# Two-layer graph and expert network, one core: filler products on TensorE in the graphs without a shared expert

## The chip, the cores and the metric

The kernel runs on one core of one Trainium2 chip. The metric is the device time of one execution in microseconds. The engines that matter here are TensorE (PE), VectorE (DVE) and ScalarE (ACT); GpSimd (POOL) does normalisation scalars and scatters, SyncE (SP) issues loads. "Granted clock" is the share of TensorE's full clock that the chip let it have in a stretch, as the profiler records it: 1.00 is 2.4 GHz, 0.50 is 1.2 GHz.

## The reference

The whole program is two layers of graph network and expert network over 16 graphs of 512 nodes with 256 features. The change lies in the third of its four parts, the attention over the graph's edges, into which the shared expert of the fourth part has been woven:

```python
def _L1_gnn_ref(X, A, Wp, bp, C):            # 8 heads of 32 features
    Xp = jnp.einsum('bnd,hdk->bhnk', X, Wp) + bp[None, :, None, :]
    Xc = jnp.einsum('bhnk,hjk->bhnj', Xp, C)
    attn = jnp.tanh(A[:, None] * jnp.einsum('bhnj,bhmj->bhnm', Xc, Xp))
    Xh = jnp.einsum('bhnm,bhmk->bhnk', attn, Xp)
    return jax.nn.relu(jnp.moveaxis(Xh, 1, 2).reshape(X.shape[0], X.shape[1], -1))
...
# in _L1_ffn_ref
shared = jax.nn.silu(xf @ sw1) * (xf @ sw3) @ sw2
```

## The kernel before

Four phases follow one another: the first graph network, the first experts, `attention_phase`, and the second experts with the final sums. Only `attention_phase` is touched. It takes the graphs b = 0 to 15 in order, and a graph in eight units u = 0 to 7, each with two halves c = 0 and 1. A unit is one block of 128 tokens for four of the eight heads. The work of a half unit goes round three engines:

- PE computes `scores` (L1408, 32 rows by 512 columns, six products) into half of the four banks `c_p_s`;
- DVE multiplies them with the adjacency in `products` (L1901, into `c_att`, two buffers that alternate by unit);
- ACT takes the tanh in place (L1699);
- PE sums the heads' outputs in `values` (L1421) once per unit, one unit behind.

The order on each engine is written out by hand. On PE a half unit is: wait for the product of DVE, `scores` of the next unit, then in half 0 `side_a(u)` and `values(u-1)`, in half 1 `side_b(u)`. The side functions hold everything else: the next graph's transposes and projections (`turn` L1428, `wide` L1440, `turn_back` L1434, `project_c` L154 to L156), the router of the graph before (`logits` L1452), the count of expert members (`count_before` L937 and L939), and the shared expert: `wide` with `ws1` and `ws3` in units 5, 6 and 7, and `down` (L1459) in units 0 and 1 of the graph after. They use three PSUM banks, `c_p_w[0..2]`; z and w name the two that swap with the graph's parity.

The shared expert is computed here for the first eight graphs alone (`OWN = 8`):

```python
going_up, going_down = post and b - 1 < OWN, late and b - 2 < OWN
```

`post` is true from graph 1 on, `late` from graph 2 on. So graphs 1 to 8 hold the upward products, graphs 2 to 9 the downward ones, and from graph 9 (10 for units 0 and 1) those places are empty. The other graphs' shared expert is computed in a later phase.

DVE's `products(b, h, u, c)` at c = 0 has two waits: `av_done` of two units before, that is until `values` has read the buffer `c_att` that it will overwrite, and `s_done`, its scores. DVE's own side work stands behind the two products of a unit.

Of the kernel before, what the change touches and what calls it, by code (L numbers as in the profile page):

```python
# [42 lines left out]
GRP = 2  # L43
# [1118 lines left out]
def attention_phase(nc, a, m, sb):  # L1162
# [3 lines left out]
    with ExitStack() as ctx:  # L1166
# [233 lines left out]
        def _(pe):  # L1400
# [36 lines left out]
            def wide(w, f, src, bank, done, last_of=False):  # L1437

                for k in range(KD):
                    mm = pe.matmul(p_s[:, bank, :] if last_of else p_w[:, bank, :], w[:, k, f * P:(f + 1) * P], src[:, k, :],  # L1440
                                   start=(k == 0), stop=(k == KD - 1))
                mm.then_inc(done, 1)
# [13 lines left out]
            def down(c, bank):  # L1456
# [3 lines left out]
                                       start=(i == 0), stop=(i == KHS - 1))  # L1460
                mm.then_inc(down_done, 1)

            def project_first():

                pe.wait_ge(xn_ready, 1)
                turn(xn, 0, 1, tr_done)
                turn(xn, 1, 2, tr_done)
                pe.wait_ge(xt_ready, KD)
                pe.wait_ge(s_w, 16 * NL)
                pe.wait_ge(init, 4)  # L1470
                wide(wp, 0, xt, 0, xpt_done)
                wide(wp, 1, xt, 1, xpt_done)
                pe.wait_ge(xpt_ready, 1)
                turn_back(xpf[:, 0], 2, xp_done)
                pe.wait_ge(xp_ready, 1)
                pe.wait_ge(xpt_lo, 1)
                pe.wait_ge(cd_split, 2)
                project_c(0, 0, 2)
                pe.wait_ge(xpt_ready, 2)
                pe.wait_ge(xpt_lo, 2)  # L1480
                project_c(0, 1, 0)
                pe.wait_ge(xct_lo, 1)
                turn_back(xpf[:, 1], 2, xp_done)
                scores(0, 0, 0, 0)
                scores(0, 0, 0, 1)

            def graph(q, h, first, last):
                b = 2 * q + h
                post = not is_at(b, 0)
                late = post and not is_at(b, 1)  # L1490
                going_up, going_down = post and b - 1 < OWN, late and b - 2 < OWN
                z, w = h, 1 - h

                def side_a(u):
                    if u == 0 and late:
                        pe.wait_ge(member_ready, b - 1)
                        if going_down:
                            pe.wait_ge(sh_ready, KHS * (b - 2) + 2)
                        else:
                            pe.wait_ge(xp_ready, GRP * b + 2)  # L1500
                        count_before(pe, m, count, member, count_done)
                    if u == 1 and post:
                        pe.wait_ge(ot_ready, GRP * b)
                        if late:
                            pe.wait_ge(r2_step, R2 * (b - 2) + 2)
                        else:
                            pe.wait_ge(xp_ready, GRP * b + 2)
                        turn_back(ot[:, 1], 2, back_done)
                    if u == 2 and not last:
                        pe.wait_ge(xn_ready, b + 2)  # L1510
                        if going_down:
                            pe.wait_ge(x4_ready, TB * (b - 2) + 1)
                        else:
                            pe.wait_ge(xct_lo, GRP * b + GRP)
                        turn(xn, 0, z, tr_done)
                        if post:
                            pe.wait_ge(x3_ready, GRP * b)
                        else:
                            pe.wait_ge(xp_ready, GRP)
                        turn(xn, 1, 2, tr_done)  # L1520
                    if u == 3 and post:
                        pe.wait_ge(xn3_ready, b)
                        if last:
                            pe.wait_ge(xct_lo, GRP * b + GRP)
                        turn(xn3[:, 1 - h], 0, z, tr3_done)
                        turn(xn3[:, 1 - h], 1, 2, tr3_done)
                    if u == 4 and not last:
                        pe.wait_ge(xpt_ready, GRP * (b + 1) + 1)
                        if post:
                            pe.wait_ge(xt3_ready, KD * b)  # L1530
                        turn_back(xpf[:, 0], 2, xp_done)
                    if u == 5:
                        pe.wait_ge(ot_ready, GRP * b + 1)
                        if not last:
                            pe.wait_ge(xpt_ready, GRP * (b + 1) + 2)
                        turn_back(ot[:, 0], z, back_done)
                    if u == 6 and going_up:
                        pe.wait_ge(x3_ready, GRP * b + 1)
                        wide(ws3, 0, xt3, z, up_done)
                    if u == 7 and going_up:  # L1540
                        pe.wait_ge(xp_ready, GRP * (b + 1) + 2)
                        wide(ws1, 1, xt3, 2, up_done)

                def side_b(u):
                    if u == 0 and going_down:
                        pe.wait_ge(hs_ready, KHS * (b - 1))
                        pe.wait_ge(xct_lo, GRP * b + GRP)
                        down(0, z)
                    if u == 1 and going_down:
                        down(1, w)  # L1550
                    if u == 2 and not last:
                        pe.wait_ge(xt_ready, KD * (b + 2))
                        if going_down:
                            pe.wait_ge(x4_ready, TB * (b - 1))
                        elif post:
                            pe.wait_ge(x3_ready, GRP * (b - 1) + 1)
                        else:
                            pe.wait_ge(xpt_ready, GRP)
                        wide(wp, 0, xt, w, xpt_done)
                    if u == 3 and not last:  # L1560
                        if post:
                            pe.wait_ge(xt3_ready, KD * (b - 1) + 1)
                        wide(wp, 1, xt, z, xpt_done)
                    if u == 4 and post:
                        pe.wait_ge(xt3_ready, KD * b)
                        if last:
                            pe.wait_ge(x3_ready, GRP * (b - 1) + 1)
                        logits(xt3, w)
                    if u == 4 and not last:
                        pe.wait_ge(xp_ready, GRP * (b + 1) + 1)  # L1570
                        pe.wait_ge(xpt_lo, GRP * (b + 1) + 1)
                        project_c(1 - h, 0, 2)
                    if u == 5 and going_up:
                        pe.wait_ge(sg_ready, b)
                        wide(ws1, 0, xt3, w, up_done)
                    if u == 5 and not last:
                        pe.wait_ge(xct_lo, GRP * (b + 1) + 1)
                        turn_back(xpf[:, 1], 2, xp_done)
                    if u == 6 and not last:
                        pe.wait_ge(xpt_lo, GRP * (b + 1) + 2)  # L1580
                        if going_up:
                            pe.wait_ge(sh_ready, KHS * (b - 1) + 1)
                        elif post:
                            pe.wait_ge(sg_ready, b)
                        project_c(1 - h, 1, w)
                    if u == 7 and going_up:
                        pe.wait_ge(hs_ready, KHS * (b - 1) + 1)
                        wide(ws3, 1, xt3, z, up_done)

                for u in range(UNITS):  # L1590
                    for c in range(2):
                        pe.wait_ge(prod_ready, 2 * (UNITS * b + u) + c + 1)
                        if u + 1 < UNITS:
                            if u + 1 == T and c == 0:
                                pe.wait_ge(xct_lo, GRP * b + 2)
                            scores(b, h, u + 1, c)
                        elif not last:
                            scores(b + 1, 1 - h, 0, c)
                        if c == 0:
                            side_a(u)  # L1600
                            if u > 0:
                                values(b, h, u - 1)
                            elif post:
                                values(b - 1, 1 - h, UNITS - 1)
                        else:
                            side_b(u)
# [762 lines left out]
```

## Time and profile before

| | |
|---|---|
| median of 3 runs | 2244.68 us (2244.51 to 2255.48) |
| profiled execution, its own time | 2249.72 us |
| span of its instructions | 2247.9 us |
| mean granted TensorE clock over the span | 0.935 |
| PE, DVE, ACT, POOL busy | 2065.9, 1537.5, 1249.5, 1065.9 us |
| attention phase, first to last product of DVE | 1022.4 to 1755.3 us of the span |

The profiled execution is 5.0 us longer than the median of the timed ones. PE's busy time includes the latency of each product, so 92% busy is not 92% of what PE could do. A unit is measured here from the start of DVE's first product of that unit to the start of the first product of the next unit.

### The profile page before, as it was taken

The page shows a single profiled execution, that of the slowest core. Times are in us where ns is not written, and L with a number is a line of the kernel's source. Part 1 is how long each engine was busy: PE and PEld are TensorE (multiplying, and loading weights), DVE is VectorE, ACT ScalarE, POOL GpSimd, SP SyncE. Part 2 cuts the span into 40 slices and gives each one's busy share as a digit, 9 for nine tenths or more (in the row PEclk, how much of TensorE's full clock was granted, in tenths as well). Part 3 has the DMA queues.
Part 4 walks back from the last instruction along what each step waited for, and adds up shares of the span by engine and source line. Part 5 has one row for each costly group of instructions (what it writes and reads, how often), then busy time and mean ns, then how long its engine had stood idle before and what let it go on. Part 6 is the DMA issues. An engine that isn't in the chain of part 4 may idle for free. (4 is left out here: it accounts for less than half of the span.)

```text
span 2247.9 us, 38345 instructions
## 1 busy us (share of the span) xinstructions
PE 2065.9 (92%) x12128; PEld 1509.9 (67%) x12128; DVE 1537.5 (68%) x3332; ACT 1249.5 (56%) x1870; POOL 1065.9 (47%) x1266
## 2 busy tenths in 40 slices
PE   7999999947999999958999999998999789999986
PEld 6988888846888888843444444444444478878853
DVE  6777777744666666645777778767776557767759
ACT  4444444404666666646676666755655357767630
POOL 3455555541333333326455545556432447777740
PEclk9999999968999999988999999978776899999998
DMA  7444445124555555542232112222210055655559
GB/s 286 147 169 167 170 170 179 44 103 149 180 179 179 177 178 180 179 158 96 73 118 80 60 60 78 82 91 70 71 66 32 6 174 182 189 166 191 184 195 355
DMA packets 138147, 315.40 MB, mean 140 GB/s; under 512 B 36990, under 2 KB 67808, under 8 KB 133952
## 3 DMA queue, kind: packets, MB, share of 16 engines
q1 hardware_dynamic: 106560, 271.77, 36.1%
q0 software_dynamic: 31488, 42.39, 5.5%
q8 instruction: 53, 0.87, 0.2%
q14 instruction: 46, 0.38, 0.1%
HBM read 206.67 MB, written 151.56 MB: 159 GB/s over the span
## 5 line engine op out<-in xcount | busy, mean ns | idle before, releaser
L1699 ACT ACTIVATE c_att<-c_att 128x1024 f32<-128x1024 f32 x256 | 270.5, 1057 | 214.0 <-DVE c_att L1901 212.1
L1901 DVE TENSOR_TENSOR c_att<-c_p_s,adj 128x1024 f32<-128x1024 f32 x256 | 302.4, 1217 | 104.5 <-PE c_p_o L1421 87.9
L2228 POOL DMA_INDIRECT moe_y<-d_y,d_goal x256 | 257.4, 1006 | 115.9 <-ACT d_y L2193 51.2
L995 POOL DMA_INDIRECT moe_y<-b_y,b_goal x144 | 156.7, 1088 | 325.5 <-DVE b_y L1047 291.7
L1408 PEld LDWEIGHTS c_p_s<-c_xcth,c_xpth 32*128 32x128 f32 x512 | 51.5, 199 | 224.6 <-issue 132.7
L154 PE MATMUL b_p_y<-b_w2h,b_hh 128*128 128x256 f32 x576 | 168.9, 293 | 6.4 <-DVE b_hl L160 3.5
L476 POOL DMA_INDIRECT moe_in<-a_xn,a_rows x128 | 141.6, 1107 | 57.6 <-issue 29.2
L1408 PE MATMUL c_p_s<-c_xcth,c_xpth 32*128 32x512 f32 x512 | 140.2, 546 | 29.4 <-DVE c_att L1901 28.5
L1421 PE MATMUL c_p_o<-c_att,c_xp 128*32 128x512 f32 x1024 | 161.5, 708 | 2.2 <-ACT c_att L1699 1.2
L160 DVE TENSOR_TENSOR b_hl<-b_ht,b_hh 128x512 fp32r<-128x512 f32 (+1 forms) x160 | 101.6, 639 | 88.7 <-ACT b_ht L1153 88.6
L155 PE MATMUL b_p_y<-b_w2l,b_hh 128*128 128x256 f32 x576 | 160.6, 279 | 0.0
L156 PE MATMUL b_p_y<-b_w2h,b_hl 128*128 128x256 f32 x576 | 160.5, 279 | 0.0
L1364 POOL DMA_INDIRECT moe_in<-c_xn,c_rows x128 | 131.1, 1024 | 53.8 <-issue 39.3
L1330 POOL TENSOR_SCALAR c_nm<-c_mv 128x4 f32<-128x4 f32 x32 | 8.2, 256 | 257.0 <-DVE c_mv L180 256.8
L160 DVE TENSOR_TENSOR d_xl<-d_p_tr,d_xh 128x1024 fp32r<-128x1024 f32 x64 | 78.4, 1225 | 75.1 <-ACT d_xh L2183 75.1
L154 PE MATMUL b_p_h<-b_xh,b_w1h 128*128 128x512 f32 (+1 forms) x320 | 121.4, 379 | 7.2 <-DVE b_w1l L160 4.8
L156 PE MATMUL b_p_h<-b_xh,b_w1l 128*128 128x512 f32 (+1 forms) x320 | 120.6, 377 | 0.0
L155 PE MATMUL b_p_h<-b_xl,b_w1h 128*128 128x512 f32 (+1 forms) x320 | 120.5, 377 | 0.0
L154 PEld LDWEIGHTS b_p_y<-b_w2h,b_hh 128*128 128x128 f32 x576 | 108.0, 188 | 16.5 <-DVE b_hl L160 15.1
L1148 ACT ACTIVATE b_w2h<-b_w 128x1024 fp32r<-128x1024 f32 x40 | 42.5, 1063 | 135.7 <-PE b_p_y L156 121.5
L1152 ACT ACTIVATE b_hh<-b_p_h,b_b 128x512 fp32r<-128x512 f32 (+1 forms) x160 | 103.8, 649 | 23.0 <-PE b_p_h L156 10.4
L1313 POOL TENSOR_SCALAR c_g<-c_g,c_ggate 128x256 f32<-128x256 f32 x120 | 110.9, 945 | 5.9 <-DMA c_g<-moe_y 3.1
(271 smaller groups left out, 6143.0 us busy)
## 6 DMA issues: line engine op xcount, KB each, us to landing
b_w<-in_moe_w SPq DMA_DIRECT2D x80, 512.0 KB, 6.1
moe_in<-b_zeros SPq DMA_DIRECT2D x65, 520.0 KB, 10.9
d_xin<-moe_in SPq DMA_DIRECT2D x64, 520.0 KB, 3.6
adj<-in_adj SPq DMA_DIRECT2D x32, 1024.0 KB, 5.4
b_xin<-moe_in SPq DMA_DIRECT2D x32, 520.0 KB, 5.9
c_g<-moe_y SPq DMA_DIRECT2D x32, 512.0 KB
moe_y<-c_zeros SPq DMA_DIRECT2D x32, 512.0 KB, 6.8
d_w<-in_moe_w SPq DMA_DIRECT2D x64, 256.0 KB
```

The source lines that it names most:

```text
L154: pe.matmul(out, lh, rh, start=start, stop=False)
L155: pe.matmul(out, lh, rl, start=False, stop=False)
L156: return pe.matmul(out, ll, rh, start=False, stop=stop)
L160: return dve.tensor_tensor(low, whole, high.bitcast(F32), ALU.subtract)
L476: pool.indirect_dma_start(out=m["moe0_in"], out_offset=bass.IndirectOffsetOnAxis(ap=rows[:, h, k, t:t + 1], axis=0), in_=xn2[:, h, t, :], ...
L995: pool.indirect_dma_start(out=m["moe0_y"], out_offset=bass.IndirectOffsetOnAxis(ap=goal[:, h, t:t + 1], axis=0), in_=y[:, h, t, :], in_off ...
L1364: pool.indirect_dma_start(out=m["moe1_in"], out_offset=bass.IndirectOffsetOnAxis(ap=rows[:, par, k, t:t + 1], axis=0), in_=xn3[:, par, t, ...
L1408: mm = pe.matmul(p_s[:, i, :], left[r, s, tok], right[r, f, :], start=(n == 0), stop=(n == 2))
L1421: mm = pe.matmul(p_o[DH * i:DH * i + DH, :], xp[:, par, t, col:col + DH], att[:, u % 2, i, :], start=(t == 0), stop=(t == T - 1))
L1699: act.activation(part, part, ACT.Tanh).then_inc(att_ready, 1)
L1901: dve.tensor_tensor(att[:, u % 2, 2 * c:2 * c + 2, :], p_s[:, 2 * c:2 * c + 2, :], adj[:, h, u % T, :].unsqueeze(1).broadcast_to([P, 2, N] ...
L2228: pool.indirect_dma_start(out=m["moe1_y"], out_offset=bass.IndirectOffsetOnAxis(ap=goal[:, h, t:t + 1], axis=0), in_=y[:, h, t, :], in_off ...
```

## The change

A function `keep_busy(bank)` is added on PE. It multiplies the 128 x 128 identity (as weights) with 512 columns of `xt3`, in f32, into one bank of `c_p_w`, and signals nobody; nobody reads the result before the bank is written anew. It is called five times per graph: in `side_a(6)`, `side_a(7)` and `side_b(7)` in graphs 9 to 15, and in `side_b(0)` and `side_b(1)` in graphs 10 to 15. That makes 7 x 3 + 6 x 2 = 33 products. Nothing else is changed: no instruction of another engine, no semaphore value.

```diff
+            def keep_busy(bank):
+
+                pe.matmul(p_w[:, bank, :], ident, xt3[:, 0, :], start=True, stop=True)
...
                     if u == 7 and going_up:
                         pe.wait_ge(xp_ready, GRP * (b + 1) + 2)
                         wide(ws1, 1, xt3, 2, up_done)
+                    if u == 6 and post and not going_up:
+                        pe.wait_ge(x3_ready, GRP * b + 1)
+                        keep_busy(z)
+                    if u == 7 and post and not going_up:
+                        keep_busy(z)
 
                 def side_b(u):
...
                     if u == 7 and going_up:
                         pe.wait_ge(hs_ready, KHS * (b - 1) + 1)
                         wide(ws3, 1, xt3, z, up_done)
+                    if u == 7 and post and not going_up:
+                        keep_busy(z)
+                    if u < 2 and late and not going_down:
+                        keep_busy(w)
```

PE's instructions before, in unit 7 of graph 9, the first graph without upward products: the scores of the next graph's unit 0 half 0, the values of unit 6, the scores of the next graph's unit 0 half 1:

```order
L1408 MATMUL c_p_s<-c_xcth,c_xpth 128x512 x2
L1408 MATMUL c_p_s<-c_xctl,c_xpth 128x512 x2
L1408 MATMUL c_p_s<-c_xcth,c_xptl 128x512 x2
L1421 MATMUL c_p_o<-c_att,c_xp 32x512 x4
L1408 MATMUL c_p_s<-c_xcth,c_xpth 128x512 x2
L1408 MATMUL c_p_s<-c_xctl,c_xpth 128x512 x2
L1408 MATMUL c_p_s<-c_xcth,c_xptl 128x512 x2
```

They follow one another without anything between. The difference at the same place:

```order
 L1408 MATMUL c_p_s<-c_xctl,c_xpth 128x512 x2
 L1408 MATMUL c_p_s<-c_xcth,c_xptl 128x512 x2
-L1421 MATMUL c_p_o<-c_att,c_xp 32x512 x4
-L1408 MATMUL c_p_s<-c_xcth,c_xpth 128x512 x2
-L1408 MATMUL c_p_s<-c_xctl,c_xpth 128x512 x2
-L1408 MATMUL c_p_s<-c_xcth,c_xptl 128x512 x2
+L1465 MATMUL c_p_w<-c_xt,consts 128x512
+L1421 MATMUL c_p_o<-c_att,c_xp 32x512 x4
+L1408 MATMUL c_p_s<-c_xcth,c_xpth 128x512 x2
+L1408 MATMUL c_p_s<-c_xctl,c_xpth 128x512 x2
+L1408 MATMUL c_p_s<-c_xcth,c_xptl 128x512 x2
+L1465 MATMUL c_p_w<-c_xt,consts 128x512
```

One filler now stands between the scores and the values of unit 6, and one behind the last scores of the graph. In unit 6 one stands in the same way between scores and values. In units 0 and 1 of graph 10 a filler follows the second half's scores, here in unit 0:

```order
 L1408 MATMUL c_p_s<-c_xctl,c_xpth 128x512 x2
 L1408 MATMUL c_p_s<-c_xcth,c_xptl 128x512 x2
+L1465 MATMUL c_p_w<-c_xt,consts 128x512
 L1408 MATMUL c_p_s<-c_xcth,c_xpth 128x512 x2
 L1408 MATMUL c_p_s<-c_xctl,c_xpth 128x512 x2
```

Nothing has changed places; the fillers only push back what stands behind them on PE.

## Rows read from the trace of the kernel before

A row of windows has: start and end (us), length, then busy us and count of PE, PE's weight loads, DVE, ACT and POOL, then granted clock, share of the DMA engines and GB/s. A row of a timeline has: start, us until the last of the group ends, engine, line, operation, tiles, and in brackets the idle time before it and what ended it.

**Rows 1.** The page: granted clock in tenths, 40 slices of 56.2 us.

```profile
PEclk9999999968999999988999999978776899999998
```

**Rows 2.** Busy time by windows: graph 8; 9; 10 to 14; 15.

```profile
1386.32:1433.09 46.77, 46.08 (x261) 22.53 (x261) 37.28 (x76) 31.71 (x43) 25.65 (x36) 1.00 0.21 69
1433.09:1478.24 45.15, 43.32 (x249) 21.33 (x249) 36.43 (x76) 29.35 (x40) 22.64 (x33) 0.93 0.26 86
1478.24:1717.27 239.03, 224.97 (x1137) 103.36 (x1139) 166.56 (x353) 141.13 (x195) 108.75 (x154) 0.76 0.22 72
1717.27:1755.30 38.03, 35.35 (x183) 16.23 (x183) 25.81 (x54) 19.22 (x23) 10.46 (x15) 0.68 0.02 4
```

**Rows 3.** Graph 12: units 0, 1, 2, 3 to 5, 6, 7, by windows.

```profile
1573.35:1579.12 5.77, 5.77 (x27) 2.38 (x27) 3.10 (x5) 4.08 (x7) 1.70 (x2) 0.50 0.01 4
1579.12:1585.81 6.69, 6.57 (x30) 2.92 (x30) 4.84 (x11) 2.71 (x4) 0.00 (x0) 0.60 0.43 151
1585.81:1591.70 5.89, 4.64 (x24) 2.41 (x26) 4.72 (x8) 3.40 (x5) 5.38 (x9) 0.71 0.02 8
1591.70:1610.06 18.36, 18.36 (x113) 9.45 (x113) 12.83 (x31) 13.02 (x20) 8.33 (x13) 1.00 0.50 150
1610.06:1614.52 4.46, 3.30 (x17) 0.82 (x16) 3.74 (x15) 2.49 (x3) 3.69 (x6) 0.70 0.09 27
1614.52:1621.18 6.66, 6.66 (x25) 2.75 (x27) 4.83 (x9) 2.60 (x3) 6.37 (x10) 0.50 0.00 0
```

**Rows 4.** Graph 1, units 0 and 1; graph 10, units 6 and 7.

```profile
1060.36:1063.67 3.31, 2.80 (x22) 1.07 (x22) 2.35 (x3) 1.99 (x3) 0.00 (x0) 1.00 0.01 2
1063.67:1069.68 6.01, 4.33 (x30) 1.88 (x30) 4.75 (x12) 4.47 (x8) 0.00 (x0) 1.00 0.42 136
1518.47:1522.27 3.80, 2.53 (x20) 1.12 (x20) 3.65 (x15) 2.49 (x3) 3.35 (x7) 1.00 0.05 13
1522.27:1526.90 4.63, 4.08 (x27) 1.62 (x23) 4.56 (x9) 2.49 (x3) 4.63 (x6) 1.00 0.00 0
```

**Rows 5.** Waits between 1478 and 1717 us: total us, times, longest us.

```profile
DVE c_att L1901 <- PE c_p_o L1421: 37.3, 27, 4.1
```

**Rows 6.** PE's timeline, graph 10, end of unit 5 to unit 0 (start, us, group, idle before).

```profile
1519.74 0.50 PE L1408 MATMUL c_p_s<-c_xcth,c_xpth 32*128 32x512 f32 x2 [1.36 <-DVE c_att L1901]
...
1520.63 1.06 PE L1421 MATMUL c_p_o<-c_att,c_xp 128*32 128x512 f32 x8
...
1525.99 0.40 PE L1408 MATMUL c_p_s<-c_xcth,c_xptl 32*128 32x512 f32 x2
1528.16 0.49 PE L1408 MATMUL c_p_s<-c_xcth,c_xpth 32*128 32x512 f32 x2 [1.77 <-DVE c_att L1901]
```

**Rows 7.** PE's timeline, two f32 products of 512 columns, in graph 10.

```profile
1498.86 3.78 PE L1440 MATMUL c_p_w<-c_xt,c_wp 128*128 128x512 f32 x4
...
1506.37 1.98 PE L1440 MATMUL c_p_w<-c_xt,c_wp 128*128 128x512 f32 x4
```

**Rows 8.** PE's timeline, graph 11, where unit 6 begins (1562.24 us).

```profile
1563.52 0.50 PE L1408 MATMUL c_p_s<-c_xcth,c_xpth 32*128 32x512 f32 x2 [1.16 <-DVE c_att L1901]
...
1564.69 1.94 PE L1421 MATMUL c_p_o<-c_att,c_xp 128*32 128x512 f32 x8
```

**Rows 9.** DVE's timeline, graph 11, unit 2: products, own places, next product.

```profile
1537.98 2.32 DVE L1901 TENSOR_TENSOR c_att<-c_p_s,adj 128x1024 f32<-128x1024 f32 x2
...
1542.05 0.69 DVE L1872 TENSOR_REDUCE c_ownpos<-c_own 128x8 f32<-128x512 f32 x1
1543.90 2.36 DVE L1901 TENSOR_TENSOR c_att<-c_p_s,adj 128x1024 f32<-128x1024 f32 x2 [1.16 <-PE c_p_o L1421]
```

**Rows 10.** PE's timeline, graph 12, transposes at either clock.

```profile
1587.06 0.50 PE L1408 MATMUL c_p_s<-c_xcth,c_xpth 32*128 32x512 f32 x2 [1.36 <-DVE c_att L1901]
...
1587.95 1.97 PE L1428 MATMUL c_p_w<-consts,c_xn 128*128 128x128 f32 x8
1589.85 1.77 PE L1421 MATMUL c_p_o<-c_att,c_xp 128*32 128x512 f32 x8
1591.55 0.50 PE L1408 MATMUL c_p_s<-c_xcth,c_xpth 32*128 32x512 f32 x2
```

## The prediction

> **What bounds the kernel now.** I read the page first: the line that departs from the rest is the granted clock, which sags to 6 to 8 tenths in slices 27 to 31, the last third of the attention phase [rows 1]. Then I cut the phase by graph. Graph 8, with the shared expert, takes 46.77 us at clock 1.00. Graphs 10 to 14 are without it, which is four pairs of f32 products less on the upward side alone, 7.9 us at full clock [rows 7], yet they take 239.03 us for five, 47.8 each, at a clock of 0.76; graph 15 takes 38.03 at 0.68 [rows 2]. So the work that left was paid back as a slower clock.
>
> Graph 12 shows where. Units 3 to 5 run at 1.00; in unit 6 the clock falls (0.70), units 7 and 0 are at 0.50, and it comes back for good only in unit 2 [rows 3]. There PE is busy all the time (5.77 of 5.77 us, 6.66 of 6.66), and DVE is not (3.10 and 4.83): at half clock PE sets the pace, and the waits say so, 37.3 us of DVE's products waiting for `values`, in 27 places [rows 5]. The same units at full clock are shorter: unit 6 3.80 and unit 7 4.63 in graph 10, unit 0 3.31 and unit 1 6.01 in graph 1 (graph 1 has no count of members, about a microsecond more of PE's and DVE's work in unit 0) [rows 4].
>
> Ahead of the fall PE waits for DVE: in graph 11 1.16 us before the first scores of unit 6, and by the next values the instructions are at half speed (1.94 us for a group that takes 1.06 at full clock) [rows 6, 8]. In graph 10 the same gap (1.36 us) passed and the clock stayed [rows 4, 6]. So this gap is at the edge: whether the clock falls depends on what lies around it and on where it happens to be caught.
>
> **The change part by part.** 33 products are added, none removed. Two such f32 products took 1.98 us at full and 3.78 at half clock [rows 7], so one filler costs PE 0.96 us at full and 1.86 at half (the row's last latency taken off). Five per graph are 4.8 us of PE at full clock, against the 7.9 us and more that the shared expert put there.
>
> I take a graph like 12 and assume full clock throughout.
> - *Units 6 and 7* (3 fillers). In graph 10 they take 3.80 + 4.63 = 8.43 us, with DVE never waiting; PE works without pause from 1519.74 to 1526.4 and then idles 1.77 us [rows 4, 6]. The fillers need 2.9, so 1.1 us more than that idle time. The filler of unit 6 pushes the values that DVE's next product waits for from 1521.69 to 1522.65, against the 1522.27 at which that product started: 0.4 us. The rest is absorbed by DVE's members work. I take 8.95 us; now 4.46 + 6.66 = 11.12 [rows 3]. Gain 2.15.
> - *Unit 0* (1 filler). PE arrives 1.1 us late from the third filler, then scores, count and values, some 2.5 us, must be done before DVE's product of unit 1. I estimate 4.4 us, that is graph 1's 3.31 plus the 1.1; now 5.77. Gain 1.35.
> - *Unit 1* (1 filler). PE has room here: graph 1 has 4.33 of 6.01 us busy [rows 4]. The filler of unit 0 stands ahead of scores and of the transposes that DVE's `add_attention` waits for, 0.1 us. 6.1 us; now 6.69. Gain 0.6.
> - *Unit 2*. Bound by DVE at full clock: two products and the own places, 1537.98 to 1542.74, 4.8 us [rows 9]; what came on top was a 1.16 us wait for values at half clock. Now 5.89. Gain 1.05.
> - *Units 3 to 5* are at full clock already and get no filler. The wait on `x3_ready` ahead of unit 6's filler costs nothing: DVE does that `add_attention` ahead of the product that the scores just before the filler have waited for.
>
> Sum: 5.1 us per graph, 42.7 instead of 47.8. Five graphs: 25.5. Graph 9 loses its clock only at its end (0.93 over the graph [rows 2]): 0.8. Graph 15 (0.68) has four of its units at half clock; by the units' gains above 4 to 5. All told 31 us if the clock never falls.
>
> It will fall, I think. The wide gap at the start of unit 6 lies *ahead* of that unit's filler (scores at 1519.74, filler at 1520.63), and nothing is put into unit 5. So the cause that took the clock down in graph 11 is untouched. Price of one such fall: unit 6 at 0.70 took 4.46 instead of 3.80, 0.66 [rows 3, 4], and the filler in it costs 0.9 more; 1.5 us. With one fall in each of the five graphs: 42.7 + 1.5 = 44.2, a gain of 25.5 - 7.5 = 18. Graph 9 then gains nothing, graph 15 some 1.5 (units 2 to 4 have no filler and, with no next graph, little other work). Sum 19.5 us: from the profiled execution's 2249.7 to 2230.2, and from the median, 5.0 us lower, **2225 us**.
>
> One thing could speak against all of it. In graph 12 the clock was at half while eight identity transposes ran from 1587.95 on, the values behind them were faster (1.77 us against 1.94), and the scores at 1591.55 are at full speed again [rows 10]: so a stretch made of identity products and values brought the clock back. The Trainium skill (TensorE: Matmul & The Clock Gate, Part 4: PE-mode transpose) says that work in transpose mode does not count as PE busy in the same way. The filler is a plain product whose weights are the identity, and by that rule taken broadly it would not hold the clock; the trace does not agree with the broad reading, and the sum goes by the row.
>
> **The rivals.**
> - *The clock never falls* in graphs 9 to 15. For it: graph 10's gap passed without filler [rows 6]. Against: graphs 11 to 14 all fell there. 2249.7 - 31, or 2214 against the median. Chance 15%.
> - *Two falls per graph*: also in unit 1 to 2, where the last filler comes before, not in, PE's wait for DVE's statistics. For it: in graph 12 the scores at 1587.06, after 1.36 us of idle, run at full clock and the transposes behind them at half (1.97 us for eight): a fall in unit 2 [rows 10]. Each costs some 1.5 to 2.5 us more: 12 us of the gain lost, 2237. Chance 12%.
> - *The clock comes back too late*, only in unit 1. Then the three fillers of units 6 and 7 and that of unit 0 are run at half clock on an engine that sets the pace, 1.86 us each, and only the one in unit 6 finds PE idle for a microsecond: some +6.5 per graph, against 1.65 saved in units 1 and 2 and about 2.5 of unit 0 and 7. Net 2 to 3 us per graph, 2257: slower. It decides at unit 7: the clock must be back before the second filler. Chance 5%.
> - *The fillers do not count as work* for the clock. All stretches stay at half, and four of five fillers are added to them: 4 x 1.86 = 7.4 per graph, about 38 over the phase, 2283. Rows 10's stretch speaks against it. Chance 4%.
> - *Nothing moves*: the time stays within 0.5%, since what is won is lost again in longer fillers. Chance 4%.
>
> **How the numbers follow.** The likeliest case, 60%, has its own range from 2217 to 2234: zero to two short falls per graph, and a few microseconds up or down in what follows the phase, where the clock also changes several times. The range reaches to 2214 below and 2238 above and leaves out the two slower cases and part of the nothing case. A measurement of this kernel tells about 0.5% (11 us) from no change. Faster by more than that, below 2233.5: all 15 points of the case without a fall, 57 of the 60, and 8 of the 12 of two falls (whose 2237 may be a few microseconds off): 80%. Within 0.5%: 11%. Slower: 9%.
>
> **What would show it.** In the changed profile: PEclk of slices 27 to 31 at 9 tenths; mean clock over the span about 0.96 to 0.97; graphs 10 to 14 at 43 to 45 us each with clock above 0.9; units 6 and 7 about 9 to 10.5 us together, unit 0 about 4.4, unit 2 under 5.3; DVE's wait for `values` down from 37 us to under 12. 33 more product groups at the filler's line, at 0.6 us an instruction. Any remaining fall begins at the start of unit 6 and is over in unit 7. It is wrong if the clock still reads 0.50 through units 7 and 0, or if full-clock units 7 and 0 are not shorter than now, which would mean that the fillers bind PE more than I count.

## The result, and the profile after

| | before | changed |
|---|---|---|
| median | 2250.08 us (2244.51 to 2255.97, 4 runs) | 2228.74 us (2224.77 to 2230.89, 4 runs) |
| profiled execution | 2249.72 us | 2230.89 us |
| mean granted clock | 0.935 | 0.960 |
| graphs 9 to 15, first product of 9 to last of 15 | 322.21 us | 301.66 us |

The change makes the kernel faster: ratio 0.9899, interval [0.9873, 0.9925], 1.0% or some 21 us. The forecast was 2225 from 2244.68, a ratio of 0.9912; a fourth run of the kernel before moved its median to 2250.08. Ratios here and below are worked out from all runs of both kernels, not from the two medians, whose quotient can differ by up to 0.002. On one chip one execution of the kernel with transposes took 5925.93 us and one of the kernel before 5506.20; neither enters a ratio, and nothing here explains them.

The page of the changed kernel, granted clock in tenths over 40 slices of 55.7 us, answers to [rows 1]:

```profile
PEclk9999999977999999987999999998998899999998
```

The sag of slices 27 to 31 is gone; what is left of it are 8 tenths in slices 28 and 31. Busy time by windows of the changed kernel (columns as in [rows 2]): graph 9; 10; 11; 12; 13; 14; 15; and 10 to 14 together:

```profile
1436.94:1481.54 44.60, 42.77 (x253) 21.10 (x253) 36.66 (x75) 29.24 (x40) 22.74 (x34) 1.00 0.27 87
1481.54:1530.18 48.64, 46.19 (x239) 20.06 (x239) 34.98 (x73) 27.84 (x39) 28.00 (x39) 0.86 0.24 78
1530.18:1572.38 42.20, 40.01 (x239) 18.38 (x239) 34.54 (x72) 27.74 (x39) 21.47 (x32) 1.00 0.29 91
1572.38:1614.57 42.19, 40.01 (x239) 18.38 (x239) 34.18 (x73) 27.75 (x39) 26.20 (x37) 1.00 0.29 94
1614.57:1658.33 43.76, 41.59 (x239) 18.62 (x239) 34.18 (x73) 27.74 (x39) 22.22 (x32) 0.96 0.19 61
1658.33:1702.14 43.81, 41.64 (x239) 18.43 (x239) 30.59 (x64) 27.73 (x39) 10.88 (x15) 0.96 0.19 65
1702.14:1738.60 36.46, 33.88 (x191) 15.16 (x189) 25.73 (x54) 19.22 (x23) 10.46 (x15) 0.86 0.02 5
1481.54:1702.14 220.60, 209.44 (x1187) 93.88 (x1187) 168.46 (x353) 138.80 (x195) 108.77 (x153) 0.95 0.24 78
```

The last row stands against 239.03 us at 0.76. Two of the five graphs keep the full clock from end to end and take 42.2 us each; graphs 13 and 14 have a short fall (43.8), graph 10 a long one (48.6).

Graph 12 of the changed kernel by unit, by windows: units 0, 1, 2, 3 to 5, 6, 7. It answers to [rows 3]:

```profile
1572.38:1576.68 4.30, 4.30 (x29) 1.75 (x29) 3.00 (x4) 2.97 (x4) 3.98 (x5) 1.00 0.01 2
1576.68:1582.76 6.08, 6.08 (x34) 2.50 (x34) 4.74 (x11) 3.49 (x6) 0.00 (x0) 1.00 0.44 144
1582.76:1587.43 4.67, 3.66 (x27) 1.96 (x28) 4.64 (x7) 2.89 (x4) 4.16 (x8) 1.00 0.09 39
1587.43:1605.41 17.98, 17.98 (x111) 9.13 (x109) 13.68 (x31) 13.41 (x21) 9.97 (x14) 1.00 0.50 155
1605.41:1609.76 4.35, 3.18 (x20) 1.06 (x20) 3.75 (x15) 2.49 (x3) 3.57 (x6) 1.00 0.07 19
1609.76:1614.56 4.80, 4.80 (x27) 1.97 (x29) 4.36 (x8) 2.49 (x3) 4.51 (x7) 1.00 0.02 3
```

PE is busy all of units 7, 0 and 1 here too, 4.80, 4.30 and 6.08 us, but at full clock: the fillers have made the place that was bound by a slow PE into one bound by a fast PE with more to do.

The long fall, in PE's timeline of the changed kernel, graph 10 (columns as in [rows 6]):

```profile
1516.07 0.66 PE L1408 MATMUL c_p_s<-c_xcth,c_xpth 32*128 32x512 f32 x2 [1.43 <-DVE c_att L1914]
...
1517.51 2.08 PE L1465 MATMUL c_p_w<-c_xt,consts 128*128 128x512 f32 x2
1519.52 1.94 PE L1421 MATMUL c_p_o<-c_att,c_xp 128*32 128x512 f32 x8
...
1526.11 2.08 PE L1465 MATMUL c_p_w<-c_xt,consts 128*128 128x512 f32 x2
1528.12 1.93 PE L1421 MATMUL c_p_o<-c_att,c_xp 128*32 128x512 f32 x8
1529.98 0.50 PE L1408 MATMUL c_p_s<-c_xcth,c_xpth 32*128 32x512 f32 x2
...
1530.88 1.12 PE L1465 MATMUL c_p_w<-c_xt,consts 128*128 128x512 f32 x2
```

It starts where the forecast put it, in the scores behind the wait ahead of unit 6 (0.66 us instead of 0.50, after 1.43 us of idle), and lasts until the scores at 1529.98, 0.2 us before unit 0. In graph 13 the fall starts in the same scores, in graph 14 in the filler behind them (1.89 us). Two fillers take 2.08 us each there; at full clock one takes 1.12.

And the waits of the changed kernel from 1481 to 1703 us, against [rows 5]:

```profile
DVE c_att L1914 <- PE c_p_o L1421: 23.1, 22, 3.4
```

**Where the time came from**, by spans of the two profiled executions. Graphs 9 to 15 are 20.55 us shorter: graphs 10 to 14 18.43, graph 15 1.57 (38.03 to 36.46), graph 9 0.55. What follows the phase is 2.1 us shorter. Ahead of the first filler 3.85 us are lost: the phase starts at 1024.47 instead of 1022.44 us, and graphs 0 to 8 take 412.47 instead of 410.65 us. That is no work of the change. Graph 0 shows how such a difference comes about: its clock goes up and down as well, and over the kernels below that leave it alone it took between 37.87 and 40.25 us. Sum: 3.85 - 20.55 - 2.1 = -18.8, the distance from 2249.72 to 2230.89.

### The profile page after: what moved, and what is told of

The parts are those of the page before. It is cut to its first block and busy times, and to the rows that moved or that the text cites. A ratio compares the mean times of both kernels' runs of the same rounds, so it can differ in the third digit from the quotient of the medians.

```text
span 2229.1 us, 38475 instructions
## 1 busy us (share of the span) xinstructions
PE 2052.3 (92%) x12194; PEld 1499.7 (67%) x12194; DVE 1538.2 (69%) x3332; ACT 1246.9 (56%) x1870; POOL 1062.8 (48%) x1266
## 5 line engine op out<-in xcount | busy, mean ns | idle before, releaser
L1408 PE MATMUL c_p_s<-c_xcth,c_xpth 32*128 32x512 f32 x512 | 130.0, 505 | 27.0 <-DVE c_att L1914 26.2
L1421 PE MATMUL c_p_o<-c_att,c_xp 128*32 128x512 f32 x1024 | 143.4, 633 | 0.0
```

The costliest lines, as they stand in the source:

```text
L1408: mm = pe.matmul(p_s[:, i, :], left[r, s, tok], right[r, f, :], start=(n == 0), stop=(n == 2))
L1421: mm = pe.matmul(p_o[DH * i:DH * i + DH, :], xp[:, par, t, col:col + DH], att[:, u % 2, i, :], start=(t == 0), stop=(t == T - 1))
```

## The experiments

The forecast's reading was this: the fall begins in the wait ahead of unit 6, which no filler covers, and the fillers behind it bring the clock back soon. The rivals were that a fall starts in whatever place it is caught, so that another filler only moves it; that any work of PE, however little of the array it fills, would do; that transposes would not do; and that the price of the fillers themselves is a large part of what is left. "Phase" is the length of graphs 9 to 15 in the one profiled execution of a kernel, 322.21 us before and 301.66 changed. Each kernel was timed against runs of the kernel before on its own chip, so ratios are compared, and times only within a chip. Unless something else is said the edit is one to the changed kernel.

**A sixth filler, in unit 5, ahead of the gap.**

```diff
@@ side_b(5)
+                    if u == 5 and post and not going_up:
+                        pe.wait_ge(sg_ready, b)
+                        keep_busy(w)
```

> The changed kernel with a sixth filler per graph, in half 1 of unit 5 of graphs 9 to 15, at the place where the first upward product stood. Theory A (what is left of the falls begins at PE's wait between unit 5 and unit 6, because no filler stands ahead of it): units 6 and 7 stay at clock 1.00 in graphs 9 to 14, each of these graphs takes 42 to 42.7 us, and against the changed kernel the time drops by the 9 to 10 us that the falls in graphs 10, 13 and 14 cost, to about 2219 us. Theory B (the falls that are left have another start, or come wherever they are caught): falls as many as in the changed kernel, and the filler adds up to 1 us a graph: 2229 to 2236 us.

2221.55 us (2217.94 to 2225.42) against 2248.59, ratio 0.9885 [0.9863, 0.9907]; phase 290.56. Windows of this kernel, graphs 10 to 14:

```profile
1482.01:1693.17 211.16, 204.66 (x1197) 93.78 (x1197) 167.72 (x352) 138.67 (x195) 109.19 (x154) 1.00 0.25 81
```

No graph from 9 to 14 has a fall, and each of the five takes 42.19 to 42.27 us. PE's timeline of this kernel, graph 12, end of unit 5:

```profile
1598.97 1.12 PE L1465 MATMUL c_p_w<-c_xt,consts 128*128 128x512 f32 x2
1599.93 0.60 PE L1434 MATMUL c_p_w<-consts,c_xpf 128*128 128x128 f32 x4
1600.78 0.49 PE L1408 MATMUL c_p_s<-c_xcth,c_xpth 32*128 32x512 f32 x2 [0.25 <-DVE c_att L1917]
```

In the changed kernel the same place reads

```profile
1604.87 0.65 PE L1434 MATMUL c_p_w<-consts,c_xpf 128*128 128x128 f32 x4
1606.69 0.50 PE L1408 MATMUL c_p_s<-c_xcth,c_xpth 32*128 32x512 f32 x2 [1.17 <-DVE c_att L1914]
```

The wait was 1.17 us and is 0.25; the filler has taken its place, and costs nothing: unit 5 takes 7.37 us (7.35 without it), unit 6 4.35 with and without. The place ahead of unit 6 was where the falls that were left came from: in none of the eight profiled executions of this section with a filler in unit 5 does a graph from 9 to 14 fall in unit 6. The filler both shortens PE's wait and adds work of the whole array; which of the two does it is not shown. The gain in time over the changed kernel is not shown by the timed runs: 0.9885 and 0.9899 have intervals that overlap, and the phases compared are from the shortest of four executions here (2217.94 us) and the longest of four there (2230.89).

**Only the three fillers of units 6 and 7, and only the two of units 0 and 1.**

```diff
@@ units 6 and 7 only
-                    if u < 2 and late and not going_down:
-                        keep_busy(w)
@@ units 0 and 1 only
-                    if u == 6 and post and not going_up:
-                        pe.wait_ge(x3_ready, GRP * b + 1)
-                        keep_busy(z)
-                    if u == 7 and post and not going_up:
-                        keep_busy(z)
...
-                    if u == 7 and post and not going_up:
-                        keep_busy(z)
```

> Only the three fillers of units 6 and 7 (graphs 9 to 15); none in units 0 and 1. If each place is needed where it stands (theory A): units 6 and 7 as in the changed kernel, units 0 and 1 up to a microsecond shorter at full clock, but the clock falls in units 1 to 2 of most graphs and gives 1.5 to 4 us back: 2228 to 2240 us. If the first three alone carry the gain (theory B): no falls in units 0 to 2, and 2222 to 2228 us.

> Only the two fillers of units 0 and 1 (graphs 10 to 15); none in units 6 and 7. Theory A: the fall at the start of unit 6 comes as before and nothing ends it in unit 7, so units 6 and 7 take 10 to 11 us as before; the clock comes back in unit 0 or 1, earlier than before: about 2238 to 2248 us. Theory B (any filler anywhere does it): near 2229 us. If they are met at half clock and only add to it: 2250 to 2260 us.

Units 6 and 7: 2241.43 us, ratio 0.9969 [0.9952, 0.9986]; phase 307.61. Units 0 and 1: 2243.12 us, 0.9977 [0.9961, 0.9993]; phase 310.87. Windows of graphs 10 to 14, first of the kernel with units 6 and 7:

```profile
1484.80:1710.48 225.68, 207.18 (x1167) 93.78 (x1167) 166.35 (x352) 139.25 (x195) 108.03 (x153) 0.92 0.24 76
```

then of the kernel with units 0 and 1:

```profile
1485.00:1711.46 226.46, 213.91 (x1157) 97.09 (x1159) 168.42 (x353) 140.22 (x195) 107.48 (x152) 0.85 0.24 76
```

In these two executions either part alone gives more than half of the phase's 20.6 us (14.6 and 11.3). The timed runs say less: 7.2 and 5.5 us of some 21, so less together than the change has as a whole. And they do different things. Without the fillers of units 0 and 1 a second fall appears in unit 2, in graphs 10, 11, 13 and 14 (unit 2 takes 5.46 to 5.94 us instead of 4.67): the two-falls case of the forecast, which those two fillers prevent. Without the fillers of units 6 and 7 the fall that starts in unit 6 or 7 lasts, as in the kernel before, through units 7 and 0 (6.65 us and up to 5.77 at half clock), or comes a little later, in unit 0, and ends only in unit 0 or 1; where it is unit 1, as in graphs 11 and 12, this unit takes 8.85 us, its own filler at half clock included.

The same two kernels, and the one with unit 5's filler alone at the end of this section, give the fillers' price at full clock. Unit 0 takes 4.30 us with the fillers of units 6 and 7 ahead of it, with its own filler or without, and 3.80 with none of them; unit 1 takes 6.08 us with a filler in unit 0 and 5.54 without; units 6 and 7 take 4.35 and 4.80 against 3.80 and, at full clock, 4.25 to 4.63. Together the five cost some 2 us of each graph's 42.2 (0.50 + 0.54 + 0.55 + 0.17 to 0.55).

**Fillers that fill less of the array, and transposes.**

```diff
@@ 32 of 128 rows
-                pe.matmul(p_w[:, bank, :], ident, xt3[:, 0, :], start=True, stop=True)
+                pe.matmul(p_w[:, bank, :], ident[0:DH, :], xt3[0:DH, 0, :], start=True, stop=True)
@@ eight transposes
-                pe.matmul(p_w[:, bank, :], ident, xt3[:, 0, :], start=True, stop=True)
+                for t in range(2 * T):
+                    pe.transpose(p_w[:, bank, t % T * P:(t % T + 1) * P], xt3[:, 0, t % T * P:(t % T + 1) * P], ident)
```

> All 33 fillers as in the changed kernel, of the same columns and the same time on PE, but with 32 of the 128 rows in use (the identity's first 32 rows as weights, 32 rows of xt3). 
> The changed kernel with each of its 33 fillers made of eight 128 x 128 transposes (the form of the kernel's own turn) in place of one product of 512 columns; by the rows of eight such transposes at full clock, 1.09 us, nearly the same PE time as the product's 0.96. Theory A (transposes against the identity hold the granted clock as other full-array work does): 2226 to 2233 us, one to three short falls. Theory B (work in transpose mode does not count, the rule of the Trainium skill's page TensorE: Matmul & The Clock Gate, Part 4): falls as long as with no filler and the fillers at half clock, 2250 to 2275 us, as the fillers of 32 rows gave.

32 rows: 2259.29 us (2245.64 to 2276.44), ratio 1.0048 [1.0001, 1.0096]; phase 336.34. Transposes: 2228.68 us, ratio 0.9919 [0.9899, 0.994]; phase 297.61. Windows of the kernel with 32 rows: graphs 10 to 14, then unit 7 of graph 12 and unit 0 of graph 13:

```profile
1483.29:1733.72 250.43, 234.38 (x1188) 107.59 (x1191) 166.57 (x353) 141.11 (x195) 106.03 (x150) 0.78 0.22 68
```

```profile
1624.54:1632.90 8.36, 8.36 (x28) 3.40 (x31) 4.60 (x8) 2.60 (x3) 6.37 (x7) 0.50 0.01 2
1632.90:1638.92 6.02, 6.02 (x30) 2.74 (x30) 3.10 (x5) 4.08 (x7) 0.00 (x0) 0.50 0.00 0
```

Its filler in PE's timeline of graph 10:

```profile
1521.85 1.90 PE L1465 MATMUL c_p_w<-c_xt,consts 32*128 32x512 f32 x2
```

This filler keeps PE just as busy (1.90 us at half clock; the one of 128 rows 2.08) and does not hold the clock: 0.78 against 0.95, with unit 7 at half in every graph from 9 to 14, and 1.7 us longer than at half clock in the kernel before, and unit 0 behind it at half in four of five. So the forecast's rival that fillers are no work for the clock holds in the main for a filler that uses a quarter of the rows: the time is 2259 us, not the 2283 priced, and unit 1 is at 0.85 to 1.00 where it was at 0.50 to 0.61 before. Whether it is the rows in use or something else that goes with the narrow form was not tried apart, nor was a filler with fewer columns of the array.

Windows of the kernel with transposes, graphs 10 to 14, and one of its fillers at full clock:

```profile
1482.36:1697.61 215.25, 204.03 (x1337) 108.16 (x1337) 167.70 (x352) 138.82 (x195) 107.92 (x153) 0.98 0.24 80
```

```profile
1612.45 1.09 PE L1466 MATMUL c_p_w<-consts,c_xt 128*128 128x128 f32 x8
```

They cost the same (1.09 us for eight against 1.12 for a product) and hold the clock about as well; of graphs 10 to 14 two have a fall in unit 6, one has it in unit 2 and two have none, about as with the products. The Trainium skill (TensorE: Matmul & The Clock Gate, Part 4: PE-mode transpose) says that transposes do not count as PE busy in the same way; for these, in f32 and with all 128 rows and columns, the trace does not agree. The trace calls both MATMUL, but has one record for a transpose and two for a product (264 for 264, 66 for 33), so the two are not carried out alike.

**The price of the fillers: half of each, and twice each** (both with the one in unit 5).

```diff
@@ half
-                pe.matmul(p_w[:, bank, :], ident, xt3[:, 0, :], start=True, stop=True)
+                pe.matmul(p_w[:, bank, 0:256], ident, xt3[:, 0, 0:256], start=True, stop=True)
@@ double
+                for i in range(2):
+                    pe.matmul(p_w[:, bank, :], ident, xt3[:, 0, :], start=True, stop=True)
```

> The six fillers per graph (unit 5 too), each of 256 columns in place of 512, so half the PE time. Theory A (it is the amount of work around PE's waits that decides): falls come back in some graphs, since half is too little where the wait is widest, but each full-clock graph is up to 0.5 us shorter: 2222 to 2236 us. If any small product is enough: no fall, 2217 to 2220 us.

> The six fillers per graph, each twice: 80 products in place of 40. The clock should stay at 1.00 in graphs 9 to 14 in either case; this prices a filler at full clock. Theory A (PE has little to spare beyond the six: units 6, 7 and 0 are full): the second product costs nearly its 0.96 us there and in unit 1, little in unit 5: 3.5 to 5 us a graph, 20 to 30 us over the phase, 2242 to 2252 us. Theory B (PE waits for DVE anyway and the second product is hidden too): up to 1 us a graph, 2222 to 2228 us.

Half: 2220.76 us (2218.17 to 2228.89), ratio 0.9898 [0.985, 0.9947]; phase 288.39. Double: 2247.68 us, ratio 0.9996 [0.9976, 1.0016]; phase 314.39. Graphs 10 to 14 by windows, first half, then double:

```profile
1479.09:1688.35 209.26, 197.94 (x1195) 96.08 (x1195) 166.29 (x353) 138.87 (x195) 109.43 (x155) 0.97 0.25 82
```

```profile
1485.70:1716.48 230.78, 229.98 (x1257) 105.15 (x1257) 167.99 (x352) 139.77 (x195) 106.56 (x151) 1.00 0.23 74
```

With twice the fillers the clock is full in every graph from 9 to 15, and yet the whole gain is gone: 46.15 us per graph, 4 us more than with one each. Unit by unit against six single fillers: 0.84 in unit 0, 0.85 in unit 1, 1.40 in unit 6, 0.86 in unit 7, nothing in unit 5. Where PE is busy all the time a second filler costs its whole 0.85 us; where PE waits afterwards it is free for as long as the wait lasts. The 1.40 holds both: the second filler of unit 5 finds 0.25 us of wait left, and the rest comes out in unit 6, where the scores start 1.80 us behind the unit instead of 1.27. PE's timeline with twice the fillers, graph 12, end of unit 5 (unit 6 starts at 1612.76):

```profile
1612.21 1.98 PE L1466 MATMUL c_p_w<-c_xt,consts 128*128 128x512 f32 x4
1614.03 0.60 PE L1434 MATMUL c_p_w<-consts,c_xpf 128*128 128x128 f32 x4
1614.56 0.50 PE L1408 MATMUL c_p_s<-c_xcth,c_xpth 32*128 32x512 f32 x2
```

The wait is gone.

With half fillers the graphs without a fall take 40.6 to 40.7 us, 1.5 less, but graphs 10 and 11 fall in unit 2, behind unit 1's halved filler, and not ahead of unit 6, where the wait is widest and the falls were expected.

**Full size where PE waits, half where it doesn't.** That leads to 512 columns in units 5 and 1, 256 in units 6, 7 and 0; it is called the mixed version below, and its filler in unit 5 is the one above.

```diff
-            def keep_busy(bank):
+            def keep_busy(bank, cols=512):
...
-                pe.matmul(p_w[:, bank, :], ident, xt3[:, 0, :], start=True, stop=True)
+                pe.matmul(p_w[:, bank, 0:cols], ident, xt3[:, 0, 0:cols], start=True, stop=True)
...
-                        keep_busy(z)
+                        keep_busy(z, 256)
...
-                        keep_busy(w)
+                        keep_busy(w, 512 if u else 256)
```

> A version that puts together what the runs so far showed: a full filler (512 columns) in unit 5 and in unit 1, where they stood in front of a wait and cost nothing, and half fillers (256 columns) in units 6, 7 and 0, where each full one cost up to 0.9 us. Graphs 10 to 14 at 40.6 us each if the clock holds (as the undisturbed graphs with half fillers), against 42.2 with six full ones: 2211 to 2216 us. If the half fillers of units 0 and 1 together were what let the clock fall in unit 2, unit 1's full one mends it; if not, one or two falls of 1.5 to 4 us each remain: 2216 to 2222 us.

> The mixed version once more, since its first timing fell on a chip on which every run, the kernel before among them, took some 100 us more in the phase after the attention. On a chip like the others the 37 to 40 us that it won there against the kernel before should leave 2208 to 2216 us, below the six full fillers (2221.6) and the changed kernel (2228.7). If its gain belongs to that chip, 2218 us or more.

First run: 2317.56 against 2356.46 us on its chip, ratio 0.9832 [0.9787, 0.9877]; phase 281.60, with one fall, in unit 2 of graph 11. Again on another chip: 2209.14 us (2205.24 to 2216.09) against 2248.83, ratio 0.9835 [0.9815, 0.9855]; phase 282.73. Windows of the second, graphs 10 to 14:

```profile
1477.86:1681.33 203.47, 196.08 (x1197) 93.50 (x1195) 168.28 (x354) 138.69 (x195) 109.06 (x154) 1.00 0.26 84
```

40.5 to 40.9 us per graph with no fall, 39.7 us below the kernel before: the best version, ahead of both kernels, with an interval that lies wholly below the changed kernel's.

**Fillers elsewhere in the phase.** To the six: three in graph 0, one in graph 1, two in graph 15 (with the adjacency as operand); and, to the mixed version, the two in graph 15 alone.

```diff
+                    if u < 2 and is_at(b, 0):
+                        keep_busy_early(w, h)
...
+                    if u in (2, 3) and last:
+                        keep_busy_early(w, h)
```

> The six fillers per graph and six products more where the clock is at half elsewhere in the phase: three in units 0 and 1 of graph 0, one in unit 1 of graph 1, two in units 2 and 3 of graph 15 (operand: the adjacency). Theory A (the same cause works there): graph 0 at about 35 to 37 us in place of 38, graph 1 at 43.5 to 45 in place of 46.6, graph 15 at 33.5 in place of 34.6; 2214 to 2219 us. Theory B (those units wait for DVE and ACT in long chains, so the clock costs nothing there): no difference to the six fillers, 2219 to 2223 us.

> The same with two more full products in units 2 and 3 of graph 15. Graph 15 took 34.6 us with the six fillers and 34.1 with these two more, both with full fillers elsewhere: 0.5 to 1.5 us less than the version without them, 2210 to 2216 us, which the timing may not tell apart. If graph 15 waits for DVE there, no difference.

2221.98 us (2216.78 to 2227.37), 0.9895 [0.9845, 0.9945], not to be told from the six fillers' 0.9885: the expected gain did not come. Graph 0 took 37.50 us against 38.09, graph 1 47.00 against 46.59, graph 15 34.08 against 34.61. The mixed version with graph 15's two: 2323.41 us, 0.986 [0.9817, 0.9903], not to be told from 0.9832 beside it; graph 15 took 32.76 us at clock 1.00 with the two and 32.36, also at 1.00, without them, where another execution of the same kernel had 35.23 at 0.85. What these places have to give is less than these runs can tell.

**The filler of unit 5 alone**, one per graph, seven in all.

```diff
@@ all other calls of keep_busy removed
+                    if u == 5 and post and not going_up:
+                        pe.wait_ge(sg_ready, b)
+                        keep_busy(w)
```

> Only the unit 5 filler, one per graph in graphs 9 to 15 (7 products). Theory A (all falls of the kernel before start at PE's wait ahead of unit 6, and nothing else does): the clock holds, graphs 10 to 14 near 41 us, 2212 to 2220 us. Theory B (with this gap covered, the next gaps, behind unit 7's last scores and in unit 1 to 2, take the clock down instead): falls start at unit 0 or 2, and it stays down until unit 2 or 3: 2232 to 2246 us. I hold B the likelier, 75%, from the falls in unit 2 when units 0 and 1 had no filler.

2338.36 against 2356.46 us, ratio 0.9931 [0.9902, 0.9961]; phase 297.08. Its windows, graphs 10 to 14:

```profile
1480.99:1699.37 218.38, 199.18 (x1145) 94.25 (x1145) 164.00 (x354) 139.41 (x195) 110.45 (x155) 0.90 0.24 78
```

Units 6 and 7 keep the full clock in every graph and take 3.80 and 4.25 to 4.62 us, but the next weak place falls instead: unit 2 in graphs 10, 12 and 13, units 0 to 2 in 11 and 14. So in the profiled executions one filler at the right place, free, is worth as much of the phase as the five of the change (297 against 302 us); in the timed runs 0.9931 and 0.9899 have intervals that just overlap. What is left are falls in units 0 to 2.

## Why the prediction was right, point by point

- *Full clock, a graph takes 42.7 us.* It took 42.2. The half microsecond is mostly units 3 to 5, 17.98 us for 18.36, which the forecast left as they were. Units, measured against forecast: unit 0 4.30 and 4.4; unit 1 6.08 and 6.1; unit 2 4.67 and 4.8; units 6 and 7 9.15 and 8.95. Right, with one term right by luck: unit 1 was said to cost 0.1 over graph 1's 6.01, but without a filler in unit 0 it takes 5.54, and the filler's price is 0.5.
- *One short fall per graph, 1.5 us.* The place was right: every fall in graphs 10 to 14 started at unit 6, and a filler ahead of it removed them all. A short fall costs 1.6 us (graphs 13 and 14). The number was not: three falls in five graphs, one of which lasted through unit 7 and cost 48.64 - 42.19 = 6.45 us. In sum 220.60 - 5 x 42.19 = 9.65 us against 7.5 forecast. The long one is only half of the forecast's rival of a clock that comes back too late: it was not back before the second filler, but it was before the third, so two fillers ran at half clock and not four, and the graph took 48.64 us, 0.8 more than the mean before, where the rival had 2 to 3 more. Why the same products brought the clock back within unit 6 in graphs 13 and 14 and not in graph 10 stays open.
- *Gain of graphs 10 to 14 18 us, graph 9 none, graph 15 1.5.* 18.43, 0.55 and 1.57. That 18.43 lies so near to 18 is in part luck: graphs at full clock gave 2.6 us more than forecast (28.1 for 25.5), and the falls took 2.15 more. Graph 9 had no fall, and paid for its three fillers.
- *DVE's wait for `values` under 12 us.* It was 23.1. This is the mis-sized sign: with fillers PE still sets the pace in units 7, 0 and 1, so 14.1 us are left with six fillers and no fall, and the falls add the rest. In the best version, with no fall and smaller fillers, it is 11.9 us:

```profile
DVE c_att L1917 <- PE c_p_o L1421: 11.9, 16, 2.3
```

- *Falls over in unit 7.* In graphs 13 and 14 already in unit 6, in graph 10 just before the end of unit 7. Mean clock 0.960, as forecast; each graph of 10 to 14 above 0.9 except graph 10 (0.86). That each would take 43 to 45 us fits graphs 13 and 14 alone.
- *The rivals.* Without any fall, 2214: the phase with six fillers is that case, 290.56 against 301.66, 11 us less as the two forecasts differ. Two falls per graph happen without the fillers of units 0 and 1. "Fillers do not count" is false for 128 rows and nearly true for 32.
- *A filler costs PE 0.96 us at full and 1.86 at half clock.* Where PE has no room the graph grew by 0.84 to 0.86 us for each (doubled fillers, units 0, 1 and 7), 1.40 in unit 6, with the overhang of unit 5's in it. At half clock only the long fall bears on it: its two fillers hold PE 2.01 us each, from their start to that of the next group, where one at full clock holds it 1.06.

## What to carry to other kernels

When work is taken off PE and its time does not fall, look at the granted clock by stage before the engines' shares; a stretch without work that fills the array can lose more in clock than the work cost (here 47.8 us per graph without the shared expert, 46.8 with it). If it must be filled, put the filler on PE just ahead of a wait, where it is free up to the length of the wait, before the place at which the fall begins and not behind it, and let it use all 128 rows (whether all columns of the array are needed was not tried); in a place where PE has no room each costs its full time, and too many eat the whole gain. Price the fillers by doubling and halving them.

## What the runs showed of the hardware that was not expected

- Busy time of PE did not hold the clock by itself. Fillers of 32 rows kept PE nearly as long at work as those of 128 (1.90 and 2.08 us at half clock), and left it at 0.78 over graphs 10 to 14 instead of 0.95.
- f32 transposes held the clock as well as products (0.98, ratio 0.9919 against 0.9899).
- The length of a wait did not decide alone: in the changed kernel the clock fell behind 1.43 us of idle in graph 10 and stayed behind 1.17 us in graph 12, but in the kernel before it fell behind 1.16 us and stayed behind 1.36 [rows 6, 8].
- On one chip every kernel took some 100 us more (2356 us for the kernel before), in what follows the attention phase, while graphs 9 to 15 were as fast as elsewhere: 281.60 and 282.73 us for the same kernel on both.
